# Two of 208 groups of gathered rows fetched row by row by another engine

## The reference, cut to what matters

```python
feature = feature - jnp.mean(feature, axis=0, keepdims=True)
std = jnp.std(feature, axis=0, ddof=1) + 0.0001
feature = feature / std
msg = edge_weight[:, None] * x[src]
support = jax.ops.segment_sum(msg, dst, num_segments=n)
output = support @ weight + bias
x = _layernorm(x + output, axis=-1)
```

## Time and profile before

| | us |
|---|---|
| median of 3 runs (3399.97 to 3411.76) | 3402.89 |
| the profiled execution's own time | 3413.44 |
| its span | 3411.7 |
| last product: first gather's start | 2347.9 |
| last gather's start | 3390.3 |
| POOL busy over the span | 2529.2 |
| ACT busy over the span | 1059.9 |

### The profile page before, as it was taken

The page is one execution under the profiler, slowest core; times in us unless marked ns, Lnnn a source line. Parts: engine busy times, 40 slices in busy tenths (PEclk is TensorE's granted clock), DMA queues, the critical chain, the costliest instruction groups (busy, mean ns, idle before and its releaser), DMA issues.

```text
span 3411.7 us, 47557 instructions
## 1 busy us (share of the span) xinstructions
PE 2507.6 (73%) x10659; PEld 1840.3 (54%) x10701; DVE 2299.3 (67%) x5450; ACT 1059.9 (31%) x3135; POOL 2529.2 (74%) x2706
## 2 busy tenths in 40 slices
PE   5776766666676666579999999996776665556777
PEld 4555544444344443368888888543444444444565
DVE  7989977777777677657776777786455455555455
ACT  3344333333333333245555555562000000000022
POOL 6777677777777777777777777576777777777775
PEclk8878988888988889799999999998988888887899
DMA  6554344444444444388988999454333333333344
GB/s 163 157 147 126 120 158 154 158 162 155 157 155 156 163 155 156 129 262 285 289 288 284 291 290 292 153 172 136 105 105 105 105 105 105 105 105 106 109 137 120
DMA packets 275056, 565.29 MB, mean 166 GB/s; under 512 B 55599, under 2 KB 121126, under 8 KB 274787
## 3 DMA queue, kind: packets, MB, share of 16 engines
q0 software_dynamic: 119808, 329.02, 30.8%
q1 hardware_dynamic: 146452, 223.99, 20.8%
q10 hardware_dynamic: 8528, 9.30, 0.9%
HBM read 419.19 MB, written 142.88 MB: 165 GB/s over the span
## 4 chain that ended last, share of the span: by engine, by line
POOL 49%; PE 22%; issue 18%; DVE 7%; DMA 2%; ACT 1%; DVEq 1%; SPq 0%; POOLq 0%; ACTq 0%
POOL arena L630 23%; POOL messages L560 21%; PE ps L1152 11%; PE ps L962 8%; POOL arena L554 5%; PE ps L1185 2%; PE ps L1085 1%; DMA messages<-arena 1%; DVE ps L2037 1%; DVE ps L2036 1%; DMA arena<-messages 1%; ACT arena L739 0%; DVE bn L2018 0%; DVE ps L1605 0%; DVE ps L1606 0%
## 5 line engine op out<-in xcount | busy, mean ns | idle before, releaser
L560 POOL DMA_INDIRECT messages<-arena x832 | 803.8, 966 | 264.1 <-issue 249.0
L554 POOL DMA_INDIRECT arena<-in_x,arena x832 | 792.1, 952 | 272.3 <-issue 250.7
L630 POOL DMA_INDIRECT arena<-x_table,wh x832 | 790.0, 950 | 263.2 <-issue 253.4
L1222 PE MATMUL ps<-arena 128*128 x2048 | 603.0, 450 | 367.0 <-SPq L505 366.7
L1222 PEld LDWEIGHTS ps<-arena 128*128 128x128 f32 x2048 | 439.4, 223 | 536.6 <-issue 469.8
L962 PE MATMUL ps<-arena 128*128 128x128 f32 x3328 | 457.8, 296 | 127.6 <-ACT arena L676 89.9
L739 ACT ACTIVATE arena<-ps,arena 128x256 f32<-128x256 f32 x832 | 326.5, 475 | 703.3 <-PE ps L1085 466.0
L962 PEld LDWEIGHTS ps<-arena 128*128 128x128 f32 x3328 | 436.8, 209 | 193.1 <-ACT arena L676 128.9
L1085 PE MATMUL ps<-arena 128*128 128x256 f32 x1664 | 470.7, 434 | 49.6 <-DVE arena L1789 42.2
L2212 DVE TENSOR_TENSOR node_a<-node_a,ps 128x256 f32 x256 | 107.7, 421 | 503.7 <-PE ps L1222 501.6
L1085 PEld LDWEIGHTS ps<-arena 128*128 128x128 f32 x1664 | 364.2, 221 | 78.9 <-issue 23.9
(11 more groups left out here) (287 smaller groups left out, 2981.9 us busy)
## 6 DMA issues: line engine op xcount, KB each, us to landing
arena<-messages SPq DMA_DIRECT2D x464, 260.0 KB
arena<-in_x SPq DMA_DIRECT2D x304, 128.0 KB, 2.8
gate_rows<-arena SPq DMA_DIRECT2D x49, 384.0 KB, 2.4
arena<-gate_rows SPq DMA_DIRECT2D x49, 384.0 KB, 3.0
arena<-in_x,arena POOLq DMA_INDIRECT x832
messages<-arena POOLq DMA_INDIRECT x832, 2.5
arena<-x_table,wh POOLq DMA_INDIRECT x832, 2.8
arena<-in_x SPq DMA_DIRECT2D x48, 256.0 KB, 2.9
```

The source lines that it names most:

```text
L554: nc.gpsimd.indirect_dma_start(out=big[:, s, j, 0:D], out_offset=None, in_=x, in_offset=bass.IndirectOffsetOnAxis(ap=ids[:, j:j + 1], axis ...
L560: nc.gpsimd.indirect_dma_start(out=messages, out_offset=bass.IndirectOffsetOnAxis(ap=ids[:, j:j + 1], axis=0), in_=big[:, s, j, :], in_off ...
L630: nc.gpsimd.indirect_dma_start(out=last_rows[:, (g + 1) % LAST_ROWS, j * D:(j + 1) * D], out_offset=None, in_=x1_table, in_offset=bass.Ind ...
L1222: last = nc.tensor.matmul(ps[g % LAST_SUMS][:, 0:D], last_hot[h][:, j, :], last_rows[:, bass.ds(k, 1), j * D:(j + 1) * D].rearrange("p o d ...
```

## The change: rows of groups 150 and 195 by ACT's queue

POOL skips groups 150 and 195. ACT fetches their 1024 rows: it loads each row's number into a register and issues a plain DMA for that row. For this SP copies the numbers of the two groups to HBM and back as one row on one partition, during the gates stage. Each of the two groups has a buffer of its own, so there are ten. A part's buffer can then no longer be read from the count's lowest bits; DVE packs both into one number (count in the low 8 bits, buffer above), and PE unpacks them. ACT begins when x1 is stored: 144 rows of group 150 ahead of the squares, eight behind each of the 24 squares, the last 176 behind the root, and then all 512 of group 195. The semaphores of x's loads, long idle by then, also count these rows, under a new name.

```diff
+LATE = (150, 195)
...
+        BUFFERS = LAST_ROWS + len(LATE)
+        last_rows = arena[:, BACK_W:BACK_W + BUFFERS * CPG * D].rearrange("p (k c) -> p k c", k=BUFFERS)
...
+        def late_rows(engine, i, first, last):
+            for r in range(first, last):
+                p, j = r // CPG, r % CPG
+                v = engine.value_load(late_row[0:1, i * GE + r:i * GE + r + 1]).with_bounds(min_val=0, max_val=NT * P - 1)
+                engine.dma_start(last_rows[p:p + 1, LAST_ROWS + i, j * D:(j + 1) * D],
+                                 x1_table[bass.ds(v, 1), :]).then_inc(S[f"rows_loaded{i}"], 16)
...
+            sp.wait_ge(S["back_kept"], 2 * PAIRS)
+            sp.wait_ge(S["back_mm"], 2 * PAIRS)
+            for i, g in enumerate(LATE):
+                sp.dma_start(late_table[i, :, :], back_id[:, g * CPG:(g + 1) * CPG]).then_inc(S["row_kept"], 16)
...
+            sp.wait_ge(S["row_kept"], 16 + 16 * len(LATE))
+            sp.dma_start(late_row, late_table.rearrange("(o i) p j -> o (i p j)", o=1)).then_inc(S["row_back"], 16)
...
             for g in range(GATHERED):
-                sp.wait_ge(S[f"second_rows{g % LAST_ROWS}"], (g // LAST_ROWS + 1) * 16 * CPG)
+                if g in LATE:
+                    sp.wait_ge(S[f"rows_loaded{LATE.index(g)}"], 16 * (2 * XPAIRS // RING + GE))
+                else:
+                    sp.wait_ge(S[f"second_rows{g % LAST_ROWS}"], rounds_of(g) * 16 * CPG)
...
             for g in range(GATHERED):
                 k = g % LAST_ROWS
+                if g in LATE:
+                    continue
...
+            act.wait_ge(S["row_back"], 32)
+            act.wait_ge(S["x1_stored"], 16 * (SPANS + 1))
+            AHEAD, EACH = 144, 8
+            late_rows(nc.scalar, 0, 0, AHEAD)
             for i in range(0, FULL // 4):
                 for s in range(2):
                     square_pair(2 * i + s, s)
+                    late_rows(nc.scalar, 0, AHEAD + EACH * (2 * i + s), AHEAD + EACH * (2 * i + s + 1))
...
+            late_rows(nc.scalar, 0, AHEAD + EACH * (FULL // 2), GE)
+            late_rows(nc.scalar, 1, 0, GE)
...
-                    rows = nc.tensor.value_load(slot_row[0:1, g:g + 1], min_val=1, max_val=GATHERED)
-                    k = (rows & (LAST_ROWS - 1)).with_bounds(min_val=0, max_val=LAST_ROWS - 1)
+                    slots = nc.tensor.value_load(slot_row[0:1, g:g + 1], min_val=1, max_val=GATHERED + (BUFFERS - 1 << ROWS_BITS))
+                    rows = (slots & ((1 << ROWS_BITS) - 1)).with_bounds(min_val=1, max_val=GATHERED)
+                    k = (slots >> ROWS_BITS).with_bounds(min_val=0, max_val=BUFFERS - 1)
...
+            link(V.tensor_copy(slot_row, parts_n))
+            link(V.tensor_scalar(buffer_i.bitcast(I32), slot_row, LAST_ROWS - 1, ROWS_BITS, ALU.bitwise_and, ALU.logical_shift_left))
+            link(V.tensor_copy(buffer_n, buffer_i.bitcast(I32)))
+            for i, g in enumerate(LATE):
+                moved = LAST_ROWS + i - (g + 1) % LAST_ROWS << ROWS_BITS
+                link(V.tensor_scalar(buffer_i, parts_n, float(g + 1), float(moved), ALU.is_equal, ALU.mult))
+                link(V.tensor_tensor(buffer_n, buffer_n, buffer_i, ALU.add))
+            link(V.tensor_tensor(parts_n, parts_n, buffer_n, ALU.add))
             link(V.tensor_copy(slot_row, parts_n))
```

More of the change, by code:

```diff
@@ L35 @@
 UNIT_BITS = 9
+ROWS_BITS = 8
 FIRST_END = E // GE
@@ L107, in gnn_program @@
         weight_row = dram("weight_row", [NT * P])
+        late_table = dram("late_table", [len(LATE), P, CPG], I32)
         node_a = sb("node_a", [P, NTP, D])
@@ L234, in gnn_program @@
         last_hot = [hot[:, k, :, :] for k in range(2)] + [area(hot_at + 2304 + k * GE, [CPG, P]) for k in range(LAST_HOTS - 2)]
-        last_rows = arena[:, BACK_W:BACK_W + LAST_ROWS * CPG * D].rearrange("p (k c) -> p k c", k=LAST_ROWS)
-        assert LAST_ROWS & LAST_ROWS - 1 == 0 and BACK_W <= 4 * D + NC and BACK_W + LAST_ROWS * CPG * D <= COLUMNS_W + 2048
+        BUFFERS = LAST_ROWS + len(LATE)
+        last_rows = arena[:, BACK_W:BACK_W + BUFFERS * CPG * D].rearrange("p (k c) -> p k c", k=BUFFERS)
+        assert LAST_ROWS & LAST_ROWS - 1 == 0 and BACK_W <= 4 * D + NC and BACK_W + BUFFERS * CPG * D <= COLUMNS_W + hot_at
         assert PARTS % (4 * RING) == 0 and PARTS <= NG
+        late_row = area(hot_at + 3840, [len(LATE) * GE], I32)[0:1, :]
         slot_row = low_tab[0:1, 0:PARTS]
+        buffer_i, buffer_n = (area(hot_at + 4928 + k * PARTS, [PARTS])[0:1, :] for k in range(2, 4))
         parts_i, parts_n = (area(hot_at + 4928 + k * PARTS, [PARTS])[0:1, :] for k in range(2))
@@ L330, in units_of, with rounds_of @@
                     (v >> UNIT_BITS).with_bounds(min_val=0, max_val=NU - NT)]
+        def rounds_of(g):
+            return sum(1 for k in range(g % LAST_ROWS, g + 1, LAST_ROWS) if k not in LATE)
+        def late_rows(engine, i, first, last):
[4 more added lines that the diff above has]
+                                 x1_table[bass.ds(v, 1), :]).then_inc(S[f"rows_loaded{i}"], 16)
         def scales_of(g):
@@ L377, in x_load @@
                 sp.dma_start(xs[:, s, :].rearrange("p (t d) -> p t d", t=2),
-                             x[2 * q * P:(2 * q + 2) * P, :].rearrange("(t p) d -> p t d", p=P)).then_inc(S[f"xs_loaded{s}"], 16)
+                             x[2 * q * P:(2 * q + 2) * P, :].rearrange("(t p) d -> p t d", p=P)).then_inc(S[f"rows_loaded{s}"], 16)
             sp.dma_start(xt[0:TAIL, :], x[FULL * P:N, :]).then_inc(S["xt_loaded"], 16)
@@ L972, in x_sum @@
             def x_sum(i, s):
-                pe.wait_ge(S[f"xs_loaded{s}"], 16 * i)
+                pe.wait_ge(S[f"rows_loaded{s}"], 16 * i)
                 nc.tensor.matmul(ps[0][:, :], ones[:, :], xs[:, s, :], start=isinstance(i, int) and i == 1 and s == 0, stop=False).then_inc(S["x_used"], 1)
@@ L1479, in run @@
                 def run():
-                    dve.wait_ge(S[f"xs_loaded{s}"], 16 * (i - X_SHIFT + XPAIRS // RING + 1))
+                    dve.wait_ge(S[f"rows_loaded{s}"], 16 * (i - X_SHIFT + XPAIRS // RING + 1))
                     mean = ps[0][:, 0:D].rearrange("p (o d) -> p o d", o=1).broadcast_to([P, 2, D])
```

## The result

| | before | after |
|---|---|---|
| median of 4 runs beside each other, us | 3401.56 | 3669.06 |
| range, us | 3399.97 to 3411.76 | 3667.32 to 3670.78 |
| ratio, 95% interval | | 1.078 [1.0766, 1.0793] |
| span of the profiled execution, us | 3411.7 | 3665.2 |

A forecast was written before the change was run, and what follows sets the result against it. POOL's 832 gathers at 1.254 us were taken to bound the last product's stage. Gathers removed -10.03 us, ACT, DVE, SP and PE 0: from 3402.89 to 3392.9 us, 8-in-10 range 3388 to 3410 us.

The forecast's parts named there:

- the size of c: Price of one row on ACT (load, register operation, one-row DMA): 0.76 us, lower end 0.52, upper end 0.86.
- Rival (a): ACT's rows are too slow and POOL stands for buffers: at 0.86 us a row, 3434 us; chance 0.13.
- rival (d): ACT's register load costs about twice what it took, 1.08 us a row, POOL stands some 192 us: 3585 us; chance 0.02.
- the slope: ACT's rows behind the root: from 0.80 us a row, each further 0.01 us costs 6.9 us.
- hidden, up to c = 0.85: ACT's 144 rows ahead of the first square end at 2457, before 2471.0; no cost up to 0.85 us a row.
- POOL's stop: If ACT is late, POOL's gathers stop at the start of group 178, at 3236 us.
- The cover: First copy of turned sums on ACT: needed at 3206, but ACT may be ready at 3232 and still cost nothing.
- The decision point of c = 0.80: ACT's 688 rows behind the root: up to 0.80 us a row they cost nothing.
- The gain: Two groups of four gathers removed from POOL in the last product: 8 x 1.254 = 10.03 us.
- POOL's own price: Slowing of POOL's gathers by 1024 more DMAs on ACT: charged nothing.
- rival (b): POOL's gathers get dearer beside ACT's DMAs, 824 x 0.016 = 13 us: 3406 us; chance 0.05.
- Rival (c): ACT a little late, PE in arrears, part of the gain given back at the end, 3 to 7 us: 3396 to 3400; chance 0.08.

The follow-up runs named there:

- three kernels: The change itself, and the change with ACT loading two or four row numbers and then issuing their DMAs: 3669.06, 3503.51 and 3409.55 us.
- batches of 8: The changed kernel with one edit, ACT loads eight row numbers and then issues their eight DMAs: 3397.93 us, ratio 0.9979.
- the kernel that fetches 640 rows: The changed kernel with 104 rows ahead of the squares, 5 behind each, and only 128 of group 195's 512 rows: 3393.08 us, ratio 0.9972.
- batches of 16: The changed kernel with sixteen loads and then sixteen DMAs in the long stretches, eight behind each square: 3392.32 us, ratio 0.9967.
- batches of four: The changed kernel with four loads and then their four DMAs: 3409.55 us, ratio 1.0023.

## Why the prediction was wrong

**The step that failed** is the size of c: "So c = 0.81 - 0.06 + 0.01 = 0.76 us", with bounds 0.52 to 0.86. Measured: 1.13 us, outside the bounds, and both signs of being wrong that hang on it came: the pitch on ACT is over 0.80 us, and POOL waits for buffers, from 3257.4 on. The pieces came from other neighbourhoods: ACT's loads of 279 ns (L769) stood behind arithmetic, SP's of 272 ns behind larger DMAs, and the one-row DMAs of 245 and 285 ns behind other DMAs. By turns they take 474 and 457 ns: 0.195 us more for the load and 0.17 to 0.21 for the DMA (against 285 and 245), 0.37 to 0.41 together, and the error is 0.37. Taking 0.06 us off for the shorter DMA went the wrong way: behind the shorter DMA the next load is longer, and on SP itself one-row pairs start 1.01 us apart where those of 128 rows had 0.81. I had no row of the pair, and treated SP's 0.86 as an upper end of ACT's price, which no row supported.

**Rival (a) and rival (d) had the mechanism.** The place, "the first copy of turned sums", the order of what stands (PE, buffers, POOL) and the point of decision came out as told for the late case, which rival (a) prices. Rival (d) came nearest in size, c = 1.08 and 3585 us, with the wrong split: it had put all of the excess into the load. Its figure is that of the Trainium skill, "DMA: Bandwidth & Descriptors", section "Latency and other measured facts", about 600 ns for a register load. Neither the page nor my row was right here: it is 474 to 477 ns behind a one-row DMA, 557 behind two of them, and 279 ns behind other loads or a DMA of 16 rows. My argument "Nothing on ACT speaks for it" gave 0.02 to a case on which the trace was silent.

**What the slope left out.** "From c = 0.80 each 0.01 us costs 6.9 us" gives (1.13 - 0.80) x 690 - 10 = +218 us at 1.13. The missing 50 us stand before the root: 144 rows take 163 us, so the first square comes at 2502.06 (31 us later than in the earlier trace rows, though the stage began 7.7 us earlier), a turn of squares takes 2520.25 - 2502.06 = 18.2 us against the mean of 16.3 that the prediction worked out, and the root is at 2721.83 where 2680.9 was forecast, 41 us late, or 49 us by the start of its own stage. My bound for that place, "hidden, up to c = 0.85", was on the safe side: at 0.95 the root is still in time, and it is passed at 1.13. The prediction's turn, 1.23 + 16 c, adds the squares' own 1.23 us to the rows; but 16 x 1.13 = 18.1 us alone fills the measured 18.2, so ACT's queue went on with the next rows while ACT squared. POOL's stop was forecast near 3236; less the 7.7 us of earlier start, and with the 27 us lost at the squares, that is 3255, and 3257.4 was measured. A slip that changes nothing: with rival (d), the chances above the range add up to 0.12, not 0.10.

**What held.** The cover: by the prediction ACT could be ready at 3232 instead of 3206, 26 us late, before POOL lost time, and three kernels give 27.9, 26.8 and 25.8 us (table above). The decision point of c = 0.80 lies between batches of 8 (0.76, nothing lost) and of 4 (0.82, 15 us lost: 0.02 x 690 = 14). The gain, 10.0 us of POOL: 8.9 us in the kernel that fetches 640 rows, 10.1 us in batches of 16 (6.8 in batches of 8, interval 4 to 10). POOL's own price of nothing: its gathers take 946 and 947 ns beside 1024 DMAs of ACT, so rival (b) is out. DVE's eight operations stay hidden: the cast now ends at 2144.17 and the first gate sum starts 0.77 us later, released by PE, as 0.8 us had been forecast (the earlier trace rows for before):

```profile
2143.89 0.28 DVE L2053 CAST low_tab<-arena 1x256 int32<-1x256 f32 x1
...
2144.94 0.75 DVE L2080 SCALAR_TENSOR_TENSOR ps<-arena,in_w,ps 128x512 f32<-128x512 f32 x1 [0.77 <-PE ps L1220]
```

Rival (c), a part given back at the end, was not seen: from the last gather to the end it is 20.0 us after and 20.1 in batches of four, where ACT was only a little late, against 21.4 before.

## What to carry to other kernels

The price of a pair of instructions is not the sum of two rows in which each stood beside its own kind: where a change makes a sequence that the trace does not have, the upper bound must be wide, or the sequence tried by itself first. On a path of a thousand such pairs a tenth of a microsecond is 100 us, so work that an engine "has time for" is to be checked at what stands behind it in its queue, with the point in c from which it decides. Where numbers are loaded into registers for one-row DMAs, load a batch of them first and issue the DMAs after: here that alone turned a loss of 267 us into a gain of 7 to 10.

## What the runs showed of the hardware

- On ACT, a register load behind a DMA of one row takes 474 to 477 ns, behind two of them 557 ns, behind another load or a DMA of 16 rows 279 ns; a one-row DMA behind a load takes 452 to 458 ns, behind another DMA 220 to 236 ns with the row's number in a register (269 ns for fixed rows back to back). A row by turns is 1.13 us, in batches of 2, 4, 8 and 16 it is 0.95, 0.82, 0.76 and 0.725 us.
- On SP the same pair is 496 + 254 ns, and its rows start 1.01 us apart.
- ACT's queue loads numbers and issues DMAs while ACT computes: 16 rows and two squares of 0.63 us take 18.2 us, and 16 x 1.13 is 18.1.
- Why the switch costs this is not visible in the records, and stays open.
- POOL's gathers did not notice any of it: 946 to 949 ns each and 0.30 us of issue, with 0 or 1024 row DMAs of ACT beside them.
